# A graph convolution on one core: GpSimd stops for TensorE's fourth radial matmul, and then waits chunk by chunk for the products

## The reference: what is computed

```
feat = node features @ W1            # a table of 12500 x 128, in HBM
h    = gelu(gelu(ea8 @ W_mlp1) @ W_mlp2)
w    = h @ [Wp_00, Wp_10, Wp_01, Wp_11]      # "radial weights", 128 an edge
mid  = products of w, feat[src] and the edge attributes ea4
n    = segment_sum(mid, dst)
out  = layernorm(x + cos(pi/8) * x @ W1_self + sin(pi/8) * n @ W2)
```

## Time and profile before

| | |
|---|---|
| median of three runs | 5436.78 us (5435.55 to 5450.42) |
| the profiled execution: its time | 5456.17 us |
| its span | 5454.4 us |
| PE busy, share of the span | 3305.5 us, 61% |
| DVE busy | 1878.1 us, 34% |
| ACT busy | 1180.1 us, 22% |
| POOL busy | 3103.3 us, 57% |
| mean granted clock of PE | 0.759 of full speed |

### The profile page before, as it was taken

One profiled execution on the slowest core, in us unless ns is written; L12 is line 12 of the kernel. 1 busy time (PEld: TensorE's weight loads), 2 busy tenths in 40 slices (PEclk: granted clock), 3 DMA queues, 4 the chain that ended last, 5 costly groups with the idle time before them and its releaser, 6 DMA issues.

```text
span 5454.4 us, 53973 instructions
## 1 busy us (share of the span) xinstructions
PE 3305.5 (61%) x15272; PEld 1812.2 (33%) x15272; DVE 1878.1 (34%) x6401; ACT 1180.1 (22%) x2646; POOL 3103.3 (57%) x3281
## 2 busy tenths in 40 slices
PE   5666656665665655666466666565665565666566
PEld 4233333332333323333233333233333333333334
DVE  2233333333333333333233333333333333333335
ACT  2122222221222212222122222121221221222124
POOL 5266566555665556556555665566566565566551
PEclk7677777777777777777777777777777777777777
DMA  6022222121221212212122222122122122222111
GB/s 151 16 46 46 44 46 45 45 44 41 46 46 43 45 41 46 46 43 46 44 42 45 45 46 44 42 47 46 42 46 46 43 46 44 45 46 46 44 44 59
DMA packets 586056, 256.03 MB, mean 47 GB/s; under 512 B 528383, under 2 KB 531867, under 8 KB 584347
## 3 DMA queue, kind: packets, MB, share of 16 engines
q0 software_dynamic: 103616, 211.52, 14.9%
q1 hardware_dynamic: 480572, 42.82, 6.7%
q10 hardware_dynamic: 1696, 0.18, 0.0%
HBM read 241.45 MB, written 12.81 MB: 47 GB/s over the span
## 4 chain that ended last, share of the span: by engine, by line
another core or an unknown queue 47%; PE 28%; issue 15%; ACT 8%; DVE 0%; ACTq 0%; DMA 0%; DVEq 0%; SPq 0%; POOL 0%; POOLq 0%
PE bank L706 7%; PE bank L716 5%; PE bank L701 5%; PE bank L749 5%; PE bank L730 3%; PE bank L741 2%; ACT h L513 2%; ACT big L518 1%; ACT ztsb L539 1%; ACT ztsb L540 1%; ACT bank L528 1%; PE bank L658 1%; ACT big L616 1%; ACT idx L497 1%
## 5 line engine op out<-in xcount | busy, mean ns | idle before, releaser
L432 POOL DMA_INDIRECT gath<-feature_table,idx x3224 | 3077.1, 954 | 2219.8 <-issue 1767.6
L716 PE MATMUL bank<-wpbd,big 128*128 128x256 f32 x3232 | 989.8, 436 | 98.4 <-issue 97.1
L958 DVE TENSOR_TENSOR big<-bank,gath 128x256 f32<-128x256 f32 x808 | 341.6, 423 | 1704.8 <-remote 1461.2
L716 PEld LDWEIGHTS bank<-wpbd,big 128*128 128x128 f32 x3232 | 711.8, 226 | 547.0 <-issue 480.0
L749 PE MATMUL bank<-ztsb,conv 128*128 128x128 f32 x1616 | 350.4, 384 | 788.8 <-ACT ztsb L540 491.2
L961 DVE TENSOR_TENSOR big<-bank,gath 128x384 f32<-128x384 f32 x1616 | 816.9, 547 | 0.0
L741 PE MATMUL bank<-ident,zsb 128*128 128x128 f32 x1616 | 340.1, 349 | 701.4 <-issue 544.6
L706 PE MATMUL bank<-h,w2bd 128*128 128x512 f32 x820 | 578.6, 795 | 259.8 <-ACT h L513 166.1
L986 DVE TENSOR_TENSOR acc<-acc,bank 128x8 f32 x3232 | 527.4, 163 | 598.5 <-remote 106.0
L701 PE MATMUL bank<-e8T,w1bd 128*128 128x512 f32 x820 | 591.9, 811 | 175.1 <-ACT big L518 90.2
L518 ACT ACTIVATE big<-bank 128x512 f32<-128x512 f32 x410 | 449.4, 1096 | 714.3 <-PE bank L706 396.7
(11 more groups left out here) (77 smaller groups left out, 756.2 us busy)
## 6 DMA issues: line engine op xcount, KB each, us to landing
gath<-feature_table,idx POOLq DMA_INDIRECT x3224
e<-in_edge_attr SPq DMA_DIRECT2D x416, 32.0 KB
ea_t<-in_edge_attr SPq DMA_DIRECT2D x100, 64.0 KB
feature_table<-gath SPq DMA_DIRECT2D x4, 1280.0 KB, 5.6
out<-big SPq DMA_DIRECT2D x4, 1280.0 KB
big<-in_x SPq DMA_DIRECT2D x3, 1280.0 KB, 8.5
dst_rows<-in_dst SPq DMA_DIRECT2D x1, 1536.0 KB
big<-in_src SPq DMA_DIRECT2D x1, 1408.0 KB
```

The source lines that it names most:

```text
L432: pool.indirect_dma_start(out=gath[:, s % SLOTS, t, :], out_offset=None, in_=table[:, :], in_offset=bass.IndirectOffsetOnAxis(ap=idx[:, s, ...
L716: last = pe.matmul(wgt_ps[c][:, 256 * r:256 * (r + 1)], h2[:, s // SUPER % 2, s % SUPER, 16 * g:16 * (g + 1), :].rearrange("q p a -> q (p ...
L958: dve.tensor_tensor(o[:, :, :, 0, :], w[:, :, :, 0, :], f[:, :, 0, :].unsqueeze(2).to_broadcast([128, n, 2, MUL]), ALU.mult)
```

## The change

Ahead of a block GpSimd waits for the fourth radial matmul of block b - 4 (`s_w[3]`) instead of that block's fourth products. Each chunk's four gathers then have a wait of their own for the products of the same chunk of block b - 4, which are the readers of the part of the slot that they write. Each of the four waits has its own increment of `s_round`, of which nobody takes notice. The first four blocks (`free` is None) are as they were.

```
     def gather_block(b, s, free, chunks=range(CHUNKS)):
         pool.wait_ge(s_idx, b + 1)
         if free is not None:
-            pool.wait_ge(s_prod[CHUNKS - 1], free)
+            pool.wait_ge(s_w[CHUNKS - 1], free)
             pool.sem_inc(s_round, 1)
         for c in chunks:
+            if free is not None:
+                pool.wait_ge(s_prod[c], free)
+                pool.sem_inc(s_round, 1)
             gather(s, c)
```

## The result

The changed kernel takes 5762.99 us (median of 4 runs, 5742.37 to 5793.09) against 5436.16 us: a ratio of 1.061 (1.0567 to 1.0653), 6% slower. The forecast was 5305 us, in a range up to 5600. The rival that ended on the slower side had given 5670 us. The profiled execution has a span of 5740.5 us, 286 us more than before. Lines behind the change are three higher: L701, L706, L716 of before are L704, L709, L719, DVE's L958 and L961 are L961 and L964, and ACT's L513, L518, L532 are L516, L521, L535.

What follows compares the result with a forecast made beforehand. The prediction took waits as the bound: POOL's 19.9 us of gathers, then a stop of about 6 us. Its terms, -317 + 74 + 150 - 38 = -131 us, gave 5305 us; own range 5200 to 5420, stated range 5100 to 5600.

Steps and rivals of the forecast that it cites:

- The rival that ended on the slower side: Stop becomes longer than what it saves, as many second gelus start beyond 18 us: 5670 us, chance 0.25.
- What the stop is: POOL's stop of about 6 us between blocks: PE's results, learned late during gathers, get through 3 us after them.
- The stop ends earlier: At 198 boundaries, waiting for the fourth radial weights instead of their products saves 1.6 us each: 317 us.
- The waits cost nothing: Four more waits and five increments a block on POOL: none ends late, taken as 0 (80 us at 0.1 us a pair).
- What is late next: PE's results fall 1.6 us later in POOL's next block; 148 blocks without transposes give back 0.5 us each, 74 us.
- its threshold: ACT's second gelu must start within 18 us of POOL's start; each us beyond lengthens the stop by one.
- The blocks with transposes: 50 blocks with one more PE result in the chain: weights 6.9 us late instead of 3.9, 150 us given back.
- The runs without a stop: Four times POOL skipped a stop, then stood still for some 20 us, costing 9.5 us each; becoming rarer gains 38 us.
- The jump of 11 us: Second gelu at 17.7 instead of 6.4 us into POOL's block, for about 1.3 us less between weights and POOL's start.

Runs made afterwards that it cites:

- e12: Kernel before with eight increments of the unused semaphore behind every gather, on a holding chip: 5300.44 us (0.9517).
- e15: Changed kernel in which POOL also pauses in mid-block until its first eight gathers have landed, on a holding chip: 5590.07 us, 1.0039 against the kernel before.
- e1: Kernel before, its stop kept, with a wait and an increment added for each chunk; on a chip that holds nothing: ratio 1.0001.
- e7: Changed kernel with 24 increments between its stop and the first gather, on a holding chip: 5613.16 us, 0.9992 against the kernel before.
- e16: Kernel before with four increments behind each gather, on a chip that holds nothing: 4216.64 us (1.0).
- e10: Changed kernel with the early stop only ahead of blocks 1 modulo 4, on a holding chip: 5715.45 us, 1.0243 against the kernel before.
- e8: Kernel before with gathers of 128 bytes a row in place of 512 (wrong results), on a holding chip: 5601.65 us (1.0023).
- e9: Kernel before with SyncE's loads in the loop cut to an eighth (wrong results), on a holding chip: 5564.13 us (0.9974).
- e13: Kernel before with POOL's indirect gathers replaced by plain transfers of 128 consecutive rows (wrong results), on a holding chip: 2715.12 us (0.4873).

## Why the prediction was wrong

*What the stop is* was right: a pause in which PE's held results get through 3 us behind POOL's last gather, and not a wait for a free slot. In the trace after, where blocks are late the third radial weights come at 2.7 to 2.9 us. e12 and, less cleanly, e15 show the same from the other side.

*The stop ends earlier* was right in size: the lead fell from 2.40 (1.63 + 0.77) to 0.86 us, 1.54 us x 198 = 305 us, against 317 in the sum.

*The waits cost nothing* was right (e1, e7, e16), by the same reasoning: satisfied waits run beside a gather. Only the first gather comes 0.09 us later (0.86 against 0.77 us).

*What is late next* is the step that failed: "For blocks without transposes [...] 148 x 0.5 = 74 us back". The mechanism was named and its threshold seen; the size of this term was wrong by a factor of six. The fourth weights came 3.55 us behind the last gather before and 6.54 after, so 2.99 x 198 = 592 us were given back, against 74 + 150 - 38 = 186 in the sum. 592 - 305 = 287 us, which is the span's 286. By kind of block, with the four runs without a stop left aside: without transposes 3.2 us behind the last gather before and 6.2 after, 3.0 x 148 = some 440 us where the sum has 74; with them 3.9 and 7.5, 3.6 x 50 = 180 us where the sum has 150. *The blocks with transposes* were sized well. The stops by class (block number modulo 4) were 8.4, 5.0, 7.7 and 8.4 us; 4.3 had been expected for the first three and over 7 for the last. 62% of all stops were over 6.9 us. ACT's second gelu of the first half came beyond 18 us of POOL's block in 142 of 194 blocks (97 of the 146 without transposes), against 19 of 194 before.

Why the price was wrong: I took it from blocks in which layer 1's matmul ended 6 to 7 us into POOL's block by chance. They were 12, nine of them with transposes and only three of the kind that was to be priced. In 11 of them every result ahead of it had been known within 1.3 us of its recorded end, so hardly anything stood in line. The term went by the place in POOL's block alone, and by that it should have come out smaller still: in the blocks without transposes this matmul moved from 4.1 to 4.9 us, and not to the 6 of the forecast. What it left out is the line. PE's results are let through in PE's order, and one that stands behind held ones waits for them too. Of the results recorded 5 to 6 us into POOL's block, those with none held ahead of them came 1.6 us late before and 3.1 after (medians), with one 3.7 and 7.0, with two 6.7 and 11.0. Two or more stood ahead of 9 of 173 such results before, and of 78 of 205 after (a tenth of PE's increments have no recorded time, so the true counts can be higher). So in the block shown a matmul only 4.6 us in was known at 12.1 us. Why the wait is longer after even with as many ahead is not shown. e10 prices one early start properly: 3 us of lateness for 1.1 to 1.5 us gained.

*The runs without a stop* became rarer as said (none of 190 boundaries in the trace after, 4 before), which was too small to matter.

*The rival* that ended slower had the place, the threshold and the order of size (5670 against 5763 us), and got a chance of 0.25. It had 40% of the ordinary blocks beyond 18 us; 66% were. Its counter-argument, that lateness doesn't feed itself, is borne out (61% of the stops behind a late block and 65% of those behind one on time were over 6.9 us) and was no help. The jump of 11 us between the earlier trace rows for 1.3 us of lead had been on the table as its evidence, and was written off as "still inside the 18 us and cost nothing". A slack that shrinks by 11 us for 1.3 us of lead, with 0.3 us left (18 - 17.7), should have made it the forecast.

## What to carry to other kernels

Before shortening a wait, ask what else gets through while it lasts. Here the stop was the time in which most of another engine's held results got through, which had nothing to do with the slot that it guarded; padding with empty instructions was worth 7%. Price a shift by moving one block of the kind in question (as e10 does), not by the blocks that happened to lie there, and ask what queues behind a late result. And look at the distance to the threshold, not at the average that lies still below it.

Of the kernels that compute the reference, e12 was the fastest on a holding chip, 4.8% faster than before. On a chip without the effect eight increments were measured only in the changed kernel, where they cost nothing.

## What the runs showed of the hardware

Chips differ. The same kernel took 5436 to 5611 us on four chips and 4216 to 4219 us on three, and a change that cost 6 to 8% on two of the first kind cost nothing where it ran, padded or with spaced gathers, on three of the second; bare, it was not run there. Whether it is the chip or its state at the time can't be told from here; within a job it never changed. The clock that PE was granted doesn't tell them apart: the mean was 0.75 to 0.76 of full speed for the kernel before on the first kind and 0.87 to 0.88 on the second, and 0.98 in e13 on a chip of the first kind.

Where it holds, only PE's results come late, and only while POOL issues indirect gathers back to back: the semaphores of DVE and ACT that the trace before has came within 0.1 us of the instruction's end, all of them. A result that is recorded within 3 us of POOL's start is known at once (85% or more in each of the three us, before and after), one at 5 to 7 us some 3 to 4 us later before the change and 7 to 8 after, and one behind 10 us nearly always not until 2.7 to 3.7 us after the last gather. The order is PE's. Bytes don't matter (e8), nor do SP's loads (e9), nor plain transfers of POOL at a still higher rate (e13: one every 0.53 us inside a block, in runs of 8.7 us). Gaps of 1 to 2.3 us between gathers let results through (e12).

The same chips also lose records: 31% of DVE's and ACT's semaphore increments in the loop have no recorded time in the trace before, 52% in e12, 1% in e1, and 5 of 6483 in e13. Every execution on record has a span and a clock from the profiler, so whether recording has a part in the holding isn't known. What in the indirect form does it stays open.

The plain form takes 537 ns of POOL for a transfer where the indirect one takes 954, so on a chip that holds nothing the gathers' 16 x 1.26 us a block set the time of the indirect kernels. With plain transfers PE, busy for 94% of the span, sets it.
